# A recommender tower on one Trainium2 core: other orders on ScalarE and GpSimd for the first chunks, idle-time matmuls in the head, and the dense columns of the top layer in one pass of high and low parts

## What is computed

```python
x0 = xk = e
for idx, (W, b) in enumerate([(w0, b0), (w1, b1), (w2, b2)]):     # W: 39 x fields_k x 128
    z = relu(einsum('bhd,bkd,hks->bsd', x0, xk, W) + b[None, :, None])
    if idx < 2:
        xk = z[:, :64]                # kept, the factor of the next layer
        direct.append(z[:, 64:])
    else:
        direct.append(z)
logit = concatenate(direct, axis=1).sum(-1)                       # 512 x 256
h = concatenate([logit, dense_ctx], axis=1)                       # 512 x 272
h = relu(h @ W_top1 + b_top1)                                     # 512 x 512
h = relu(h @ W_top2 + b_top2)                                     # 512 x 256
y = h @ W_top3                                                    # 512 x 1
```

## Time and profile before

| | |
|---|---|
| median of the runs | 683.54 us |
| the profiled execution | 687.57 us |
| its span | 685.8 us |
| PE busy | 633.7 us (92%) |
| DVE busy | 587.2 us (86%) |
| ACT busy | 252.4 us (37%) |
| POOL busy | 315.5 us (46%) |
| granted TensorE clock, mean | 0.985 |
| moved by DMA | 129.97 MB, 190 GB/s |

### The profile page before, as it was taken

One profiled execution on the slowest core, in us unless ns is written; L12 is line 12 of the kernel. 1 busy time (PEld: TensorE's weight loads), 2 busy tenths in 40 slices (PEclk: granted clock), 3 DMA queues, 4 the chain that ended last, 5 costly groups with the idle time before them and its releaser, 6 DMA issues.

```text
span 685.8 us, 5970 instructions
## 1 busy us (share of the span) xinstructions
PE 633.7 (92%) x1856; PEld 347.2 (51%) x1856; DVE 587.2 (86%) x548; ACT 252.4 (37%) x330; POOL 315.5 (46%) x391
## 2 busy tenths in 40 slices
PE   0169798979999999999999999999999999999998
PEld 0025354535555555555555555555555555555544
DVE  2049798968999999999999999999999999999920
ACT  2013335324434434343344443443434444333312
POOL 6752764746546453636464454635473131322210
PEclk9979999989999999999999999999999999999999
DMA  9689818864765849394857567584939474260100
GB/s 209 172 268 359 246 42 291 247 238 127 227 222 158 298 126 328 61 332 94 293 155 249 191 188 267 148 305 90 349 59 327 111 260 170 86 220 1 63 0 1
DMA packets 125630, 129.97 MB, mean 190 GB/s; under 512 B 59646, under 2 KB 67598, under 8 KB 125599
## 3 DMA queue, kind: packets, MB, share of 16 engines
q1 hardware_dynamic: 117679, 128.16, 57.6%
q0 software_dynamic: 5120, 1.32, 2.1%
q10 hardware_dynamic: 2800, 0.12, 0.3%
HBM read 123.18 MB, written 6.39 MB: 189 GB/s over the span
## 4 chain that ended last, share of the span: by engine, by line
PE 79%; ACT 0%; issue 0%
PE z L647 50%; PE z L637 8%; PE z L638 7%; PE z L639 7%; PE z L654 1%; PE z L711 1%; PE z L655 1%; PE top L701 1%; PE z L701 0%; PE tp L701 0%; PE top L694 0%; PE xk L717 0%; PE tp L628 0%; PE tp L630 0%; PE z L694 0%; PE tp L694 0%
## 5 line engine op out<-in xcount | busy, mean ns | idle before, releaser
L647 PE MATMUL z<-whole,w 128*128 128x512 f32 (+2 forms) x928 | 434.5, 601 | 17.0 <-DVE whole L582 16.2
L647 PEld LDWEIGHTS z<-whole,w 128*128 128x128 f32 (+2 forms) x928 | 177.5, 193 | 176.6 <-issue 156.7
L582 DVE TENSOR_TENSOR whole<-bc,xk 128x1024 f32<-128x1024 f32 (+1 forms) x208 | 231.3, 1131 | 28.6 <-PE z L647 19.5
L421 ACT ACTIVATE high<-raw 128x1024 fp32r<-128x1024 f32 (+1 forms) x128 | 135.3, 1058 | 293.4 <-DVE raw L574 238.6
L320 POOL DMA_INDIRECT emb<-in_tables,rows_all x160 | 169.7, 1060 | 54.4 <-issue 53.6
L558 DVE TENSOR_TENSOR low<-raw,high 128x1024 fp32r<-128x1024 f32 (+1 forms) x128 | 161.7, 1263 | 7.9 <-issue 4.6
L637 PE MATMUL z<-high,w_high 128*128 128x512 f32 (+1 forms) x256 | 143.5, 561 | 9.7 <-issue 5.6
L574 DVE TENSOR_TENSOR raw<-bc,xk 128x1024 f32<-128x1024 f32 x112 | 135.8, 1212 | 0.0
L338 POOL TENSOR_TENSOR stack<-stack_raw,stack 64x512 fp32r<-64x512 f32 x32 | 45.0, 1406 | 196.9 <-ACT stack L428 196.8
L638 PE MATMUL z<-high,w_low 128*128 128x512 f32 (+1 forms) x256 | 101.5, 397 | 0.0
L639 PE MATMUL z<-low,w_high 128*128 128x512 f32 (+1 forms) x256 | 101.2, 395 | 0.0
(11 more groups left out here) (55 smaller groups left out, 179.2 us busy)
## 6 DMA issues: line engine op xcount, KB each, us to landing
bc<-fields SPq DMA_DIRECT2D x64, 1024.0 KB, 5.9
rot<-fields SPq DMA_DIRECT2D x16, 1280.0 KB
bc<-fields SPq DMA_DIRECT2D x16, 768.0 KB
rot<-fields SPq DMA_DIRECT2D x16, 512.0 KB
fields<-xt SPq DMA_DIRECT2D x64, 80.0 KB
bc<-fields SPq DMA_DIRECT2D x32, 128.0 KB
rep<-fields SPq DMA_DIRECT2D x48, 80.0 KB
emb<-in_tables,rows_all POOLq DMA_INDIRECT x160
```

The lines of the kernel that those rows point to most:

```text
L421: act.activation(high[0:m, k % PART_SLOTS], raw[0:m, k % RAW_SLOTS], ACT.Copy).then_inc(high_ready, 1)
L582: nc.vector.tensor_tensor(whole[0:rows, n % WHOLE_SLOTS, 0:len(tiles)], left, right, ALU.mult).then_inc(whole_ready, 1)
L647: ins = nc.tensor.matmul(z[layer][:, :], w[layer][0:m, WHOLE_AT[layer, t], :], whole[0:m, k % WHOLE_SLOTS, u], start=(t == 0), stop=(layer ...
```

## The change

- **GpSimd**: four gathers are issued at the start and not three; gathers 3, 4 and 5 each move ahead of a `stack_part` behind which they stood. `dense` is set to zero first.
- **ScalarE**: for the first chunks, the high part of (0,1) moves ahead of `turned(2)`, the first high part of (2,0) ahead of `layer0_out(1)`, and `layer1_direct(1)` and `layer1_kept(1)` behind the high part of (0,3).
- **TensorE**: 11 fp32 matmuls of 512 columns with no use (`keep_busy`, into the bank `top[0]`) before layer 0 of chunk 0, and 2 behind it.
- **The dense columns**: `dense` and the 16 dense rows of `W_top1` are loaded three times, at partitions 0, 32 and 64. ScalarE rounds all three to fp32r; VectorE puts the low part of dense at 32 and that of the weights at 64. One fp32r matmul of 80 rows for each of the four output tiles then sums high x high, low x high and high x low. The parts of the weights lie in `w_high`, where those of layers 0 and 1 were; the rounding comes behind (1,15).

The diff, without the declarations of the semaphores:

```diff
@@ -47,7 +47,11 @@
 FOLDS = 3
+FIRST_ROWS, FIRST_KEPT = 11, 2
 H1, H2, DENSE = 512, 256, 16
+DENSE_AT = (0, 32, 64)
+DENSE_ROWS = DENSE_AT[-1] + DENSE
@@ -110,8 +114,8 @@
         logits = sb("logits", [PART, 2, BATCH])
-        dense = sb("dense", [PART, BATCH // PART, DENSE])
-        denseT = sb("denseT", [DENSE, BATCH])
+        dense = sb("dense", [PART, BATCH // PART, DENSE_ROWS])
+        dense_parts = sb("dense_parts", [DENSE_ROWS, BATCH], fp32r)
@@ -120,7 +124,9 @@
         wt1 = bc[0][:, 0:2, :]
-        wt1_dense = bc[0][0:DENSE, 2, :]
+        wt1_dense = bc[0][0:DENSE_ROWS, 2, :].rearrange("p (a s) -> p a s", s=OUT)
+        wt1_parts = w_high[0:DENSE_ROWS, 0:H1 // OUT, :]
         wt2 = bc[0][:, 3:5, :].rearrange("p a (b n) -> p (a b) n", n=H2)
@@ -297,7 +308,8 @@
             sp.dma_start(wt1[:, :, :], A["W_top1"][0:2 * OUT, :].rearrange("(t p) n -> p t n", p=PART)).then_inc(top_in, 16)
-            sp.dma_start(wt1_dense[:, :], A["W_top1"][2 * OUT:2 * OUT + DENSE, :]).then_inc(top_in, 16)
+            for row in DENSE_AT:
+                sp.dma_start(wt1_dense[row:row + DENSE, :, :], A["W_top1"][2 * OUT:2 * OUT + DENSE, :].rearrange("p (a s) -> p a s", s=OUT)).then_inc(top_in, 16)
             sp.dma_start(wt2[:, :, :], A["W_top2"].rearrange("(t p) n -> p t n", p=PART)).then_inc(top_in, 16)
@@ -305,6 +317,7 @@
         def _(pool):
+            pool.memset(dense[:, :, :], 0.0).then_inc(dense_zero, 1)
             pool.memset(ident[:, :], 0.0).then_inc(ident_zero, 1)
@@ -355,26 +368,26 @@
-            gather(0)
-            gather(1)
-            gather(2)
+            for c in range(4):
+                gather(c)
             landed(2)
+            landed(3)
             fold(0, 0)
...
             own_done()
-            gather(3)
-            landed(3)
+            gather(4)
+            landed(4)
             fold(1, 0)
...
             own_done()
-            gather(4)
-            landed(4)
+            gather(5)
+            landed(5)
             stack_part(1, 1)
...
             for p in range(1, CHUNKS + 1):
-                if p + 4 in IN:
+                if p > 1 and p + 4 in IN:
                     own_done()
@@ -393,7 +406,9 @@
                 act.dma_start(bias[:, layer:layer + 1], A[f"L0_rec_b{layer}"].rearrange("(s a) -> s a", a=1)).then_inc(small_in, 16)
-            act.dma_start(dense[:, :, :], A["dense_ctx"].rearrange("(j p) c -> p j c", p=PART)).then_inc(small_in, 16)
+            act.wait_ge(dense_zero, 1)
+            for row in DENSE_AT:
+                act.dma_start(dense[:, :, row:row + DENSE], A["dense_ctx"].rearrange("(j p) c -> p j c", p=PART)).then_inc(dense_in, 16)
             with nc.allow_non_contiguous_dma(reason="small columns"):
@@ -435,10 +450,12 @@
                     act.wait_ge(d_free[0], c)
+                else:
+                    kept(0)
                 act.activation(direct[0][0:KEEP, :], z[0][KEEP:OUT, :], RELU, bias=bias[KEEP:OUT, 0:1]).then_inc(d_ready[0], 1)
...
                     act.wait_ge(stack_ready, STACK_NO[1, c - 1] + 1)
-                kept(0)
+                    kept(0)
@@ -457,9 +474,9 @@
-            act.wait_ge(small_in, 64)
+            act.wait_ge(small_in, 48)
             act.wait_ge(dense_t, 1)
-            act.activation(denseT[:, :], top[0][0:DENSE, :], ACT.Copy).then_inc(dense_ready, 1)
+            act.activation(dense_parts[:, :], top[0][0:DENSE_ROWS, :], ACT.Copy).then_inc(dense_high, 1)
             act.wait_ge(w0_ready, 2)
@@ -478,11 +495,12 @@
             layer1_kept(0)
-            turned(2)
             for g in SPLIT[0]:
                 high_part(0, 1, g)
+            turned(2)
+            high_part(2, 0, SPLIT[2][0])
             layer0_out(1)
-            for g in SPLIT[2]:
+            for g in SPLIT[2][1:]:
                 high_part(2, 0, g)
@@ -495,13 +513,18 @@
             layer0_out(2)
-            layer1_direct(1)
-            layer1_kept(1)
...
                         high_part(0, p + 2, g)
+                if p == 1:
+                    layer1_direct(1)
+                    layer1_kept(1)
+                if p == CHUNKS:
+                    act.wait_ge(top_in, 80)
+                    act.wait_ge(stack_free, STACK_NO[1, CHUNKS - 1] + 1)
+                    act.activation(wt1_parts, wt1_dense, ACT.Copy).then_inc(top_high, 1)
                 layer2_out(p - 1)
@@ -550,6 +573,10 @@
+            lower = slice(DENSE_AT[1], DENSE_AT[1] + DENSE)
+            dve.wait_ge(dense_high, 1)
+            nc.vector.tensor_tensor(dense_parts[lower, :], top[0][lower, :], dense_parts[lower, :], ALU.subtract).then_inc(dense_ready, 1)
             pending = []
@@ -618,6 +645,9 @@
             lows(-2)
+            dve.wait_ge(top_high, 1)
+            lower = slice(DENSE_AT[2], DENSE_AT[2] + DENSE)
+            nc.vector.tensor_tensor(wt1_parts[lower, :, :], wt1_dense[lower, :, :], wt1_parts[lower, :, :], ALU.subtract).then_inc(top_parts, 1)
@@ -653,6 +683,11 @@
                 nc.tensor.matmul(z[layer][:, :], w_low[:, n, :], stack[:, :], start=False, stop=True).then_inc(stack_free, 1)
+            def keep_busy(times):
+                for _ in range(times):
+                    nc.tensor.matmul(top[0][:, :], ident[:, :], w[1][:, 0:N // OUT, :], start=True, stop=True)
@@ -670,28 +705,32 @@
             pe.wait_ge(ident_ready, 1)
-            pe.wait_ge(small_in, 64)
+            pe.wait_ge(dense_in, 48)
             for j in range(BATCH // PART):
-                ins = nc.tensor.transpose(top[0][0:DENSE, j * PART:(j + 1) * PART], dense[:, j, :], ident[:, :])
+                ins = nc.tensor.transpose(top[0][0:DENSE_ROWS, j * PART:(j + 1) * PART], dense[:, j, :], ident[:, :])
             ins.then_inc(dense_t, 1)
...
             pe.wait_ge(w_low_ready, 2)
+            pe.wait_ge(dense_ready, 1)
+            keep_busy(FIRST_ROWS)
             for layer, c in STEPS:
                 one_layer(layer, c)
+                if layer == 0 and c == 0:
+                    keep_busy(FIRST_KEPT)
                 if layer and c == 0:
...
-            pe.wait_ge(top_in, 48)
-            pe.wait_ge(dense_ready, 1)
+            pe.wait_ge(top_in, 80)
+            pe.wait_ge(top_parts, 1)
             pe.wait_ge(xt_ready, 2 * CHUNKS)
...
             for m in range(H1 // PART):
-                nc.tensor.matmul(h1_banks[m][:, :], wt1_dense[:, m * PART:(m + 1) * PART], denseT[:, :], start=True, stop=False)
+                nc.tensor.matmul(h1_banks[m][:, :], wt1_parts[:, m, :], dense_parts[:, :], start=True, stop=False)
             for at, width, last in ((0, BATCH - SUB, False), (BATCH - SUB, SUB, True)):
```

More of the change, by code:

```diff
@@ L172, in tower @@
         folded = sem("folded")
+        dense_zero = sem("dense_zero")
+        dense_in = sem("dense_in")
         dense_t = sem("dense_t")
+        dense_high = sem("dense_high")
+        top_high = sem("top_high")
+        top_parts = sem("top_parts")
         dense_ready = sem("dense_ready")
```

## The result

The changed kernel takes 677.65 us (median of 15 runs, 674.24 to 690.15) beside 684.66 us for the kernel before (15 runs, 678.96 to 687.37): a ratio of 0.9885 [0.9863, 0.9908], 7.9 us of 683.54. Four of the 15 runs of the changed kernel took 687.64 to 690.15 us, over 1.5% above its fastest, and the ratio leaves such slow runs out. The prediction was 13.9 us less, 669.6 us, with a range from 666 to 676. The sign is right, the size is not. The profiled execution took 676.74 us with a span of 674.9 us; 673.7 was predicted for it.

What follows compares the result with a forecast made beforehand. TensorE bounds the body, so only its idle time, half clock and removable work count. 0.4 + 2.0 + 7.3 + 0 + 0 + 2.6 + 1.6 = 13.9 us off 683.54 gives a median of 669.6 us, range 666 to 676.

Steps and rivals of the forecast that it cites:

- Dense landed: Head, ScalarE's queue: two more dense loads land at 13.2 us, between 10.2 and 22.0, covered, worth 0.
- The idle-time matmuls: Head of TensorE: they start at some 22.0 and end at 33.9; what they win is spent waiting for GpSimd: 0.
- The gap of (0,3): TensorE's 2.75 us gap before 120.37: ScalarE's earlier high part lets TensorE resume at 118.3, gaining 2.0 us.
- that of the first high part of (2,0): TensorE's 1.38 us gap before 81.73: closes when ScalarE's high part goes ahead of layer0_out(1).
- The dense pass: Top layers: one pass of four split matmuls takes 1.0 us instead of 3.63, gaining 2.6 us.
- the top as a whole: Top layers: 2.6 us from the shorter dense pass and 1.6 from the half clock behind it going.
- The 1.6 us of it for the clock: Top layers, 665.6 to 668.8: half clock blamed on thin 16-row matmuls goes with them, gaining 1.6 us.
- the 7.3 us of Part 1: Stack (1,2): GpSimd's earlier gathers remove TensorE's 4.49 us gap and the half clock behind it, 7.3 us.
- the 1.3 of stack (1,0): Price of GpSimd's order: gather 3 ahead of stack (1,0) makes TensorE start it at 68.2, 1.3 us late.
- C: Rival: the wait moves to stack (1,1) or (2,0), with half clock behind it: 674.4 us, chance 0.15.
- The second half of D: Rival: the gap before 144.39 is not the gather's, so its 7.3 us stay: 676.9 us, chance 0.03.
- ScalarE's order: First chunks: earlier high parts gain 1.7 us, less 1.3 for stack (1,0), or 0.4, plus 2.0 at (0,3).

Runs made afterwards that it cites:

- after_2: The changed kernel run again, unchanged, on one chip with no_busy_2: 675.38 us, ratio 0.9881 to the kernel before.
- e8_top_only: The kernel before with the dense pass alone, old orders on ScalarE and GpSimd, no idle-time matmuls: 680.85 us, ratio 0.995.
- before_3: The kernel before, unchanged, profiled a third time: 682.17 us.
- no_busy_2: The changed kernel without any idle-time matmuls, run again beside after_2 on the same chip: 674.09 us, ratio 0.9855 to the kernel before.
- e11_thick: The kernel before with three copies of dense, dense columns as four fp32 matmuls of 80 rows, no idle-time matmuls: one execution, 683.43 us.
- e9_pool_only: The kernel before with the dense pass and GpSimd's new order, ScalarE's old order, no idle-time matmuls: 677.22 us, ratio 0.9901.
- e3_no_busy: The changed kernel without any idle-time matmuls, first run: 673.70 us, ratio 0.9829 to the kernel before.
- e4_stack_vector: The changed kernel with the low part of stack (1,0) on VectorE and not GpSimd: ratio 0.9844 to the kernel before.
- before_2: The kernel before, unchanged, profiled a second time: 683.48 us.
- e1_pool_back: The changed kernel with GpSimd's old order, all else kept: ratio 0.9935 to the kernel before; its profiled execution took 686.55 us.

## Why the prediction was partly right and where it failed

**What held.** Dense landed at 13.90 (13.2 predicted) and stayed covered. The idle-time matmuls began at 22.28 and the first product came at 34.51, where 22.0 and 33.9 were said; GpSimd took back what they won. The gap of (0,3) lost 1.9 us of the 2.0 booked (0.9 in `after_2`, where 1.82 is left), and that of the first high part of (2,0) closed. Stack (1,2) has no wait and no half clock behind it. The dense pass took 0.94 us (1.0 predicted), the top as a whole 4.6 us less (4.2 predicted), and the ratio of `e8_top_only`, 0.995 (3.4 us), bears the term out in the median. The 1.6 us of it for the clock are not in every execution: in `before_3` the clock at the top did not fall, and its 12.83 us are only 2.9 more than the 9.95 of the new top. The body is unchanged. One edit I had overlooked: behind (0,0) the kept half goes ahead of the direct half. It takes the gap in front of (1,0) from 3.38 to 2.67 us (`no_busy_2`), 0.7 us, which in the kernel after the wait for GpSimd at stack (1,0) covers as well.

**The step that failed: the 7.3 us of Part 1, and with it taking the 13.9 off the median as well.** The prediction priced the gap and the half clock at stack (1,2) from one execution and took them for a property of the kernel. Two more profiles show no gap there, nor do `e8_top_only` and `e11_thick`, the other two with both old orders. GpSimd's part comes 25.1 to 29.5 us behind stack (1,1), by the length of gather 5 and its landing, and TensorE needs 25.0 to 26.5, so the wait is 4.49 us in one execution of five and nothing in the others. GpSimd's new order is worth 3.3 us in the median (`e8_top_only` to `e9_pool_only`), where 7.3 less the 1.3 of stack (1,0) was booked. The page had a sign of it: the execution stood 4.0 us above the median of the first three runs, and above every one of the 15 of the result, whose median is 684.66. I wrote this down and took the offset to stay. It did not: the execution after is 0.9 us below its own median. So 3.1 us of the miss are in the profiled executions (676.74 for 673.7) and 4.9 us in this offset; together they are the 8.0 us between 669.6 and 677.65.

By the ratios the terms of the sum come out like this. The top gave 3.4 us of 4.2. The two orders together gave 6.5 to 8.3 of 9.7 (`e8_top_only` to `no_busy_2` or `e3_no_busy`). The idle-time matmuls, booked at nothing, took 1.8 to 3.8 back, of which the smaller figure is within the intervals.

**The second step: stack (1,0).** 68.2 was predicted, 69.69 came. Gather 3 started at 47.05 and not at 46.1, took 14.1 us and not 13.6, and landed 5.24 us later and not 5. I had booked a late stack (1,0) one for one. But TensorE, idle for 4.96 us, then ran at half clock to about 79 us, which I had not booked: the stretch of 69.69 to 118.39 takes 48.7 us, that of 66.86 to 114.88 before 48.0, although two gaps in it had shrunk. Stack (1,1) is 3.5 us later than before, where 0.4 us earlier was predicted. This, too, is one execution: in `after_2` TensorE waits 1.93 us, stack (1,0) comes at 65.97 and stack (1,1) at 113.94, 0.9 us earlier than before. So the size of this step in the median is not shown.

A rule that I had weighed and turned down bears on this. The Trainium skill's GPSIMD Engine Reference, section Specifications, says that GpSimd's SBUF interfaces are shared with VectorE, with contention where VectorE has two SBUF inputs. Of the ten issues of gather 3, two took 1.84 and 1.83 us, and each began 0.21 us behind a low part of VectorE (54.41 and 57.81); the other eight took 0.94 to 1.00, though VectorE was hardly idle. The trace agrees that such slow issues exist and are worth 0.9 us each, but it does not bear out that all of them are slow.

**The rivals.** None came as written. C had the right kind of loss, an extra wait for a landing with half clock behind it, but at stack (1,0), where I had put the wait and not the clock; in `e4_stack_vector`, with that stack out of the way, C's wait appears at (2,0), 4.65 us. The second half of D, that the 7.3 us are not to be had, gives 676.9 and lies nearest to the time; its reason is wrong, since the gap was the gather's and did go. ScalarE's order was booked at 2.4 us regardless of the others; it is worth nothing with GpSimd's old order and 3 to 5 us behind the new one.

**The best versions.** Without the idle-time matmuls the kernel took 673.70 and 674.09 us, with two stack parts on VectorE besides 672.97 and 675.05. All four are faster than both kernels by their medians. Against the kernel after (0.9885, then 0.9881) the first runs give 3.7 to 3.8 us and the second, on one chip with it, 1.1 to 1.8, which is within the intervals.

## What to carry to other kernels

Before a gap of one profile is priced, compare that execution's time with the median: when it stands above it by as much as a good part of the gap, profile the kernel again, and subtract from the execution that looks like the median. Where another engine comes last at a step, follow back what started it. Here that was an earlier step of the bounding engine, so the wait is the difference of two ways from there, and an edit must shorten the longer one: ScalarE's order shortened TensorE's way, lengthened GpSimd's, and was worth nothing until GpSimd's order went with it. A wait moved onto an earlier step can also cost the clock behind it: book both.

## What the runs showed of the hardware

- Whether the clock falls behind a gap of 2.8 us differs from execution to execution of one kernel: at 73 us it held in the first profile before, fell for 3.4 us in `before_2`, and the window from 72 to 80 us is at 0.59 in `before_3`.
- GpSimd's indirect DMAs go out 1.25 us apart (0.95 and 0.30 of pause); single ones take up to 3.1 us, and three to eight of the 40 in the head take over 1.2. Their data are there 2.9 to 5.9 us behind the last issue in the head, and 1.4 to 6.1 for gathers 3 to 5 behind it.
- In two of the 18 profiled executions ScalarE began late although the TensorE work that it needed was over, 6.6 us in `e1_pool_back` (shown above; the transposes ended at 35.98) and 8.3 in the other; in `e3_no_busy` it began the kept half of (0,0) at 55.15, its product over at 46.90, and TensorE waited (ScalarE's, then TensorE's timeline of `e3_no_busy`):

```profile
55.15 1.32 ACT L447 ACTIVATE xk<-z,bias 64x512 f32<-64x512 f32 x2 [16.68 <-issue]
```

```profile
57.78 4.64 PE L677 MATMUL z<-whole,w 128*128 128x512 f32 x5 [10.89 <-issue]
```

In `no_busy_2`, the same kernel, those matmuls start at 49.18. The profiled execution of `e3_no_busy` took 684.12 us, 10 above its median. What held ScalarE is open; it may be part of the width of the intervals, and of why the ratios of small edits in the head can't be told apart here.
